# Residual sum of a Mamba block: from a VectorE add to a TensorE accumulation and a ScalarE copy

## What is computed

```
x = x + mamba(ctx, layernorm(x), ...)        # the residual sum of this change
x = x + layernorm(x) @ (sum_r factors[r]) / sqrt(8) + bias

def mamba(hidden, z, ...):
    x = silu(conv4(hidden @ in_proj_w.T) + conv_b)      # [b, 512 channels, 512 positions]
    dt_low, B, C = split(x_proj_w @ x)                  # 16, 16, 16 rows
    dt = softplus(dt_proj_w @ dt_low + dt_proj_b)
    state = state * exp(dt * A) + (dt * x) * B          # a scan over positions, 16 states a channel
    y = sum_n(state * C) + D * x
    return swapaxes(y * silu(z))                        # z: one column block of layernorm(x)
```

## Time and profile before

| what | us |
|---|---|
| median of 3 runs | 535.95 (534.97 to 536.77) |
| the profiled execution, its own time | 536.2 |
| its span, first to last instruction | 534.4 |
| VectorE busy | 484.1 (91%) |
| GpSimd busy | 438.7 (82%) |
| TensorE busy | 424.5 (79%) |
| ScalarE busy | 349.0 (65%) |
| mean granted TensorE clock | 0.92 |

### The profile page before, as it was taken

How to read it: one execution, slowest core, us unless ns; L and a number is a source line. 1 busy time by engine, 2 the same in 40 slices (tenths; PEclk the granted TensorE clock), 3 DMA queues, 4 the chain that set the end, 5 groups by cost and what they waited for, 6 DMA issues and landing times.

```text
span 534.4 us, 3951 instructions
## 1 busy us (share of the span) xinstructions
PE 424.5 (79%) x988; PEld 179.8 (34%) x1000; DVE 484.1 (91%) x390; ACT 349.0 (65%) x607; POOL 438.7 (82%) x219
## 2 busy tenths in 40 slices
PE   8625967786855958898888897889888879788997
PEld 4202322332322323333333343324333333333443
DVE  5688999999999999989999999989999999999542
ACT  2578463876539876598678875697679757555240
POOL 1037999999998899979999799979999999999100
PEclk9885979799879889899899899899898989899899
DMA  5989445444984000010591000000790000000012
GB/s 173 272 250 383 163 78 118 79 82 82 282 306 118 0 0 0 1 59 2 188 412 73 0 20 1 8 14 0 264 389 21 0 20 1 21 0 20 0 41 79
DMA packets 20287, 53.69 MB, mean 100 GB/s; under 512 B 2708, under 2 KB 2708, under 8 KB 20264
## 3 DMA queue, kind: packets, MB, share of 16 engines
q1 hardware_dynamic: 16296, 45.05, 23.8%
q0 software_dynamic: 3968, 8.39, 8.7%
HBM read 48.98 MB, written 4.46 MB: 100 GB/s over the span
## 4 chain that ended last, share of the span: by engine, by line
POOL 38%; DVE 19%; issue 18%; PE 17%; ACT 4%; DMA 3%; SPq 1%; POOLq 0%; DVEq 0%; ACTq 0%
POOL h L850 26%; DVE dA L719 10%; POOL h L843 9%; PE y L356 6%; PE work L349 4%; DVE h L719 3%; DVE h L725 3%; PE work L437 2%; DMA b_rep<-bc_scratch 2%; PE work L316 2%; POOL dtu L836 2%; ACT dA L552 1%; DVE acc L667 1%; PE work L351 1%; POOL fsum L861 1%
## 5 line engine op out<-in xcount | busy, mean ns | idle before, releaser
L850 POOL TENSOR_TENSOR h<-b_rep,dtu 128x1024 f32<-128x1024 f32 x127 | 305.2, 2479 | 10.9 <-DMA b_rep<-bc_scratch 10.6
L356 PE MATMUL y<-h,ident 128*128 128x512 f32 x512 | 260.3, 647 | 59.8 <-DVE h L725 54.3
L552 ACT ACTIVATE dA<-dt,a_neg 128x512 f32<-128x512 f32 x256 | 165.9, 680 | 111.1 <-DVE h L725 84.7
L719 DVE TENSOR_TENSOR_SCAN dA<-dA,h 128x1024 f32<-128x1024 f32 x80 | 182.8, 2285 | 2.8 <-POOL h L850 2.5
L356 PEld LDWEIGHTS y<-h,ident 128*128 128x128 f32 x512 | 100.5, 205 | 206.5 <-issue 108.8
L843 POOL TENSOR_TENSOR h<-h,c_rep 128x1024 f32<-128x1024 f32 x48 | 119.4, 2487 | 20.2 <-DVE h L719 20.2
L719 DVE TENSOR_TENSOR_SCAN h<-dA,h 128x1024 f32<-128x1024 f32 x48 | 109.5, 2281 | 9.6 <-ACT dA L552 9.1
L725 DVE TENSOR_TENSOR h<-dA,c_rep 128x1024 f32<-128x1024 f32 x80 | 97.3, 1216 | 1.1 <-DVE dA L719 0.2
L308 PE MATMUL work<-ctx_sb,w_in 128*128 128x512 f32 x60 | 33.1, 684 | 17.6 <-DVE x L739 16.0
L349 PE MATMUL work<-fsum,xnT 128*128 128x512 f32 x88 | 41.0, 609 | 0.0
L667 DVE SCALAR_TENSOR_TENSOR acc<-work,chan,acc 128x511 f32<-128x511 f32 (+2 forms) x45 | 32.3, 729 | 0.2
(11 more groups left out here) (111 smaller groups left out, 360.7 us busy)
## 6 DMA issues: line engine op xcount, KB each, us to landing
b_rep<-bc_scratch SPq DMA_DIRECT2D x32, 512.0 KB, 8.7
c_rep<-bc_scratch SPq DMA_DIRECT2D x32, 512.0 KB, 8.2
fsum<-factors POOLq DMA_DIRECT2D x8, 1024.0 KB, 9.3
x<-x SPq DMA_DIRECT2D x4, 1024.0 KB, 8.1
out<-x SPq DMA_DIRECT2D x16, 256.0 KB, 2.0
ctx_sb<-ctxT SPq DMA_DIRECT2D x3, 512.0 KB, 6.0
ctx_sb<-ctxT SPq DMA_DIRECT2D x2, 256.0 KB, 4.2
w_in<-w_inT SPq DMA_DIRECT2D x2, 256.0 KB, 4.5
```

Of the source, the lines that this page charges most:

```text
L356: mm = pe.matmul(y[:], ident[:], h[:, (s * PAIRS + j) % H_RING, i, :], start=False, stop=(j == SUM_ORDER[-1] and i == 1))
L552: act.activation(dA[:, j % 2, i, :], dt[:, k % 2, :], ACT.Exp, scale=a_neg[:, k, 2 * j + i:2 * j + i + 1]).then_inc(exp_done, 1)
L719: dve.tensor_tensor_scan(pair if j in POOL_C else decay, decay, pair, 0.0, ALU.mult, ALU.add).then_inc(scanned, 1)
L850: pool.tensor_tensor(h[:, (s * PAIRS + j) % H_RING], b_rep[:, j], dtu[:, k % 2, :].unsqueeze(1).to_broadcast([P, 2, L]), ALU.mult).then_in ...
```

## The change

TensorE first puts `x` into `work0` by an identity matmul, then accumulates the four turned blocks of `yg` on it by matmuls in place of transposes. ScalarE copies the sum to `x1`, behind decay pair 3 of the next step; for step 15 it does so straight after the loop, ahead of the copy to `l_dt` and of `t_final`. VectorE's add is taken out.

```diff
             def turn_y(s):
 
+                b, k = divmod(s, KB)
+                pe.wait_ge(x_landed, (b + 1) * 16)
+                pe.matmul(work0[:].rearrange("p (t d) -> p t d", t=KB), ident[:], x1_columns(b, k), start=True, stop=False)
                 pe.wait_ge(gated, s + 1)
                 for t in range(KB):
-                    tr = pe.transpose(work0[:, t * P:(t + 1) * P], yg[:, t * P:(t + 1) * P], ident[:])
-                tr.then_inc(y_turned, 1)
+                    mm = pe.matmul(work0[:, t * P:(t + 1) * P], yg[:, t * P:(t + 1) * P], ident[:], start=False,
+                                   stop=(t == KB - 1))
+                mm.then_inc(y_turned, 1)
...
+            def x1_evac(s):
+                b, k = divmod(s, KB)
+                act.wait_ge(y_turned, s + 1)
+                act.wait_ge(g_done, (b + 1) * KB)
+                act.activation(x1_columns(b, k), work0[:].rearrange("p (t d) -> p t d", t=KB), ACT.Copy
+                               ).then_inc(x1_added, 1)
...
+                    if j == 3 and s > 0:
+                        x1_evac(s - 1)
                     if j == 3 and k == KB - 2 and b + 1 < BATCH:
                         act.preload_act_table_set("silu_and_others")
                         silu_batch(b + 1)
...
             for s in range(STEPS):
                 act.wait_ge(dt_reset, s + 1)
                 step(s)
+            x1_evac(STEPS - 1)
             act.wait_ge(t_turned, STEPS - KB)
             act.activation(l_dt[:], work2[:], ACT.Copy).then_inc(t_xnT, 1)
             t_final_(STEPS - KB - 2)
...
-            def add_x1(s):
-                b, k = divmod(s, KB)
-                dve.wait_ge(y_turned, s + 1)
-                dve.wait_ge(g_done, (b + 1) * KB)
-                dve.tensor_tensor(x1_columns(b, k), work0[:].rearrange("p (t d) -> p t d", t=KB),
-                                  x1_columns(b, k), ALU.add).then_inc(x1_added, 1)
...
-                    if j == 3 and s > 0:
-                        add_x1(s - 1)
...
             gate_y(STEPS - 1)
-            add_x1(STEPS - 1)
             dve.wait_ge(x1_added, STEPS)
```

## The result

The kernel after takes 539.92 us, median of 18 runs (536.4 to 542.3); the kernel before took 536.53 us, median of 18 (534.97 to 537.45). The ratio is 1.006, 95% interval 1.0043 to 1.0077: 3.4 us slower, where 538.0 us and 0.4% slower were forecast, with 534.5 to 540.6 as range. The profiled execution of after took 542.3 us, span 540.5; it is the longest of the 18.

The account below looks back on a forecast made before the run. The prediction took the bound to vary by step: VectorE never waiting, VectorE waiting for ScalarE, or GpSimd. Terms -2.8 + 2.6 + 0 + 2.2 = +2.0 us gave 538.0 us, 0.4% slower, range 534.5 to 540.6.

Parts of the forecast that it names:

- The add leaves VectorE: Without the add, VectorE gains 0.46 us in each of six steps where it never waits, 2.8 us in all.
- kind (a): Steps 5, 7, 9, 13, 14 and 15, in which VectorE never waits; only there does the 0.46 us gain count.
- GpSimd's cover in steps 13 to 15: GpSimd's products with B end 3.4 us ahead of the scan, so its load costs nothing; otherwise up to 1.4 us lost.
- ScalarE's copy: In steps 4, 6, 8, 10 and 12 it delays scan 4 by 0.52 us each, 2.6 us; elsewhere in the loop hidden.
- GpSimd's steps: Steps 1, 2, 3 and 11, read as set by GpSimd, where VectorE's saved time becomes waiting.
- The copy waits for y_turned: Step 6: TensorE's turned sum is ready 0.5 us before ScalarE's copy; step 12: level; cost 0.
- The turning: TensorE's four turning matmuls, eight records of 0.11 us with loads hidden: 0.88 us, upper bound 2.4.
- the dear turning: Rival: each turning record also costs its weight load, partly or fully; 540.3 us half way, 543.5 at most; chance 0.12.
- The tail: After step 15, ScalarE's copy precedes l_dt and t_final, releasing TensorE's next last_layer 2.2 us later, all exposed.
- the new gap of TensorE: Rival: TensorE's idle time in the tail, 509.9 to 511.7, brings a low clock stretch, 1.7 us: 539.7 us; chance 0.05.
- Steps 1, 2, 3 and 11: GpSimd sets these steps, so VectorE's saved time is waited away there; gain 0.
- The clock rival: Low TensorE clock stretches at the last_layer of steps 6 and 10 vanish, 1.7 us each: 534.6 us if both; chance 0.25.

Follow-up runs that it names:

- copy_off: The kernel after without ScalarE's copy, the first layer's residual sum left out; ratio to before 0.997.
- add_off: The kernel before without VectorE's add, the first layer's residual sum left out; ratio to before 0.997.
- tail_last: The kernel after with ScalarE's last copy moved behind the copy to l_dt and t_final; ratio to before 1.0051, median 538.67 us.
- copy_behind4: The kernel after with ScalarE's copy behind decay pair 4, not 3, in even steps from 4 on; ratio to before 1.0112, median 542.84 us.
- pe_part: The kernel after with VectorE copying the sum out in place of ScalarE, in loop and tail; ratio to before 1.0022, median 537.71 us.
- shift_tt: The kernel before with the gate's shift on VectorE as one plain two-tensor product; one run, 536.19 us against 538.01 of before.
- shift_dense: The kernel before with the gate's shift in its old three-operand form but reading neighbouring elements; one run, 537.3 us against 538.01 of before.
- shift_pool_after: The kernel after with the gate's shift moved from VectorE to GpSimd; ratio to before 0.9884, median 529.78 us.
- hybrid: The kernel after, shift on GpSimd, VectorE copying in steps 2, 4, 6, 8, 10, 12 and the tail, ScalarE elsewhere; ratio to before 0.9837, median 527.86 us.

## Why the prediction held, and the step that failed

*The add leaves VectorE, 2.8 us.* Right: the six steps of kind (a) lost 0.44 to 0.46 us each, 2.7 in all, in every kernel without the add. GpSimd's cover in steps 13 to 15 held.

*ScalarE's copy, 0.52 us in five steps.* Right: +0.48, +0.51, +0.47, +0.52 and +0.56 us, 2.5 in all, and copy_off takes it back. The waits grew to 14.5 us where 14.0 were foreseen: scan 4 of step 2, which has a table switch too and was counted among GpSimd's steps, now waits 0.64 us. Step 2 reads 29.61 to 29.64 us in the four kernels with ScalarE's copy in it and 29.46 to 29.50 in the ten others.

*The copy waits for y_turned, 0.* Right: no wait stands ahead of L558 at 232.02.

*The turning, 0.11 us a record.* Right, in the loop and the tail; the dear turning fell. The Trainium skill, TensorE: Matmul & The Clock Gate, Part 3, has a line by which loads overlap matmuls only in different row groups; the prediction's estimate from it, 1.7 us for the eight, is not what these rows show: 1.05 us with a load for each. The same part also lets a load into the background weight buffer go ahead, and these rows agree with that. The half-way price of the dear turning was added up wrongly: 8 x 0.21 less 0.88 is 0.80 us, not 0.85. Nothing hangs on it.

*The tail, 2.2 us.* Right, 2.24; the new gap of TensorE (1.67 us) brought no low stretch, for the eight matmuls behind it take 3.70 us and the eight ahead of the gap 3.60.

*Steps 1, 2, 3 and 11, "time saved on VectorE earlier in those steps is waited away there", 0.* This is the step that failed, for step 11: it measured +1.22 us. In step 3 the shift did swallow the gain as foreseen (5.79 us in place of 5.33, ending at 154.17 with L840 at 152.54 + 1.60 = 154.14). In step 11 I took a shift that ended with GpSimd by luck (0.39 us) for a sign that GpSimd sets the step. VectorE waited nowhere in step 11 of before: 27.07 us is step 13's 26.89 and 0.18 for a short shift, so the step was VectorE's. The shift could only be held longer when it came at another moment, and without VectorE's add it comes 0.4 us earlier. In all five kernels without VectorE's part there (after, add_off, copy_off, tail_last, copy_behind4) it took 1.7 to 2.2 us; in before, pe_part and shift_tt 0.35 to 0.39, but 1.77 in shift_dense, whose schedule is before's. So the change makes the long one likely, and luck has a part in it; how often a kernel draws it is not known, since one execution a kernel is profiled. With shift_pool_after the step takes 26.44 us, what step 13 takes there.

*The sum.* +2.0 forecast, +3.4 measured: step 11's 1.2 and 0.3 in steps 0 to 3 were missing, with small differences in the other terms.

*The clock rival, 3.4 us less if both low stretches leave steps 6 and 10.* In the profiled execution of after they were still there, 0.53 and 0.59 at the last_layer (before 0.61 and 0.62):
```profile
222.10:225.50 3.40, 3.40 (x6) 1.44 (x5) 3.40 (x3) 3.34 (x7) 2.99 (x2) 0.53 0.00 0
342.00:345.40 3.40, 3.40 (x6) 1.47 (x5) 3.40 (x4) 3.26 (x6) 2.97 (x3) 0.59 0.00 0
```
But three of its 18 runs took 536.4 to 536.6 us at a mean clock of 0.943 to 0.955, and the other fifteen 539.0 to 542.3 at 0.926 to 0.937. The distance is the rival's price. Those three were not profiled, so that the two stretches left them is argued, not shown. Shown is the price: in add_off and copy_off step 6 reads 29.4 and step 10 28.35, without a low stretch at the last_layer, where the kernel before reads 31.07 and 30.05, 1.7 us each. Shown too is that these stretches go without the adding matmuls: add_off lost both stretches with TensorE's transposes as before, and of two kernels that differ from before by the form of the shift alone, shift_tt has no low stretch at step 10's last_layer and shift_dense none at step 6's. They come and go from execution to execution.

The forecast came out near for five terms that were right; the 1.2 us of the step that failed lay within the range by luck, for nothing in the prediction bounded what a held shift takes, and in step 3 it was 5.3 us. Had step 11 been costed by both ends of a held shift (0 and 2.4 us, a GpSimd instruction) and put between them, the forecast would have been 539.2.

## What to carry to other kernels

Moving work from the busiest engine pays only in those steps where that engine never waits, and it costs in those where the receiver does: read the waits step by step, and split the move by steps, as hybrid does. A small operation whose duration in one place is ten times that in another is a stall in disguise; moving it was worth more than the change it stood beside (6.5 us here against 3.4). Before moving the emptying of a bank, see who writes the bank next, and what stands behind whom in the tail.

## What the runs showed of the hardware

A VectorE product of 128x4 with two tensors in SBUF was held for 5.3 us, past the ends of two GpSimd instructions and to that of a third (shift_tt: from 147.34 to 152.65, over the ends at 149.11 and 151.41, to the one at 152.62):
```profile
144.18 4.93 POOL L851 TENSOR_TENSOR h<-b_rep,dtu 128x1024 f32<-128x1024 f32 x2
148.84 2.57 POOL L844 TENSOR_TENSOR h<-h,c_rep 128x1024 f32<-128x1024 f32 x1
151.13 1.49 POOL L837 TENSOR_TENSOR dtu<-dt,u 128x512 f32<-128x512 f32 x1
```
In step 11 it took 0.35 to 2.2 us by where it fell between them. With one tensor operand four of them took 0.55 us, and on GpSimd itself one took 0.20 to 0.56. The Trainium skill, SBUF — State Buffer, in "SBUF: two separate sides", has a rule for this: a port pair shared by VectorE and GpSimd is an exclusive lock, which a VectorE instruction with two SBUF inputs must take against a GpSimd one that reads SBUF, and whoever is first keeps it to its end. The four forms of the shift agree with it. That the shift is not let in at the first end is no part of what the section says.

A short idle time of TensorE in the loop of copy_behind4 cost twice over: 3.15 us of standing, and then 3.44 us for matmuls that take 1.88 in after, at a granted clock of 0.59 in place of 1.00. An fp32 matmul of 128 moving columns cost what two transposes do, 0.22 us (two records of 0.11), with its weight loads hidden.
